# Row statistics of tiles 26 to 28 from accumulating ScalarE passes, and the last tile's maximum from its centred rows

## The chip, the core and the metric

The kernel runs on one core of a Trainium2 chip. The metric is the device time of one execution in microseconds, as the median of the runs.

## The reference

A transformer block on x of 8 batches x 512 rows x 512 columns, with a context of 77 rows a batch:

```
x = x + cross_attention(layernorm(x), ctx) @ Wo + bo        # 8 heads of 64
n = layernorm(x)                                            # over the 512 columns, eps 1e-5
s = sigmoid(clip_x) * max(abs(n)) / 127                     # one scale for the whole tensor
q = clip(round(n / s), -128, 127)
h = silu(s * q @ Wg') * (s * q @ Wu')                       # Wg', Wu', Wd' rounded to 8 bits by row
h is rounded in the same way, with one scale for the whole tensor
x = x + h' @ Wd'
```

What matters here is that the scale s needs the largest absolute value of n over all 4096 rows. No row can be rounded, and no product of the feed-forward part can start, before the last row of the attention part is normalised and its maximum is known.

## The kernel before, in words

The 4096 rows are 32 tiles of 128 rows. The attention part goes through the tiles in order, and tile n of the second normalisation takes these steps: `wo(n)` on TensorE gives the output projection; `residual(n)` (L607, VectorE) adds it to the row tile and writes `x1`; `second_stats` and `second_aggr` (L613, L617, VectorE) give mean and variance; `second_scale` (L621, L623, L625, GpSimd) gives the inverse deviation `r2` and the product `mr2` = -mean x `r2`; `normed(n)` (L631, ScalarE) writes `n2` = `x1` x `r2` + `mr2`, and a DMA of SyncE's queue stores it to DRAM (`n2_rows`); `largest(n)` (L637, VectorE) writes the tile's largest absolute value to a column of `amx`. The store of `x1` to the output tensor goes through the same SyncE queue. `x1` and `n2` have four buffers each (tile n uses buffer n mod 4), so `residual(n)` waits until the store of `x1` of tile n-4 has landed, and `normed(n)` until that of `n2` has.

The order of every engine's instructions is written out by hand: `add(engine, ...)` appends to the engine's list and gives a semaphore value, and an engine runs its list in order. `last_batch()` writes out tiles 22 to 27, and a loop behind it tiles 28 to 31. Between the two stand four small ScalarE operations (L1021, called dg here), which make diagonal matrices of weight scales. The last tile is normalised on VectorE in place of ScalarE (`last_normed`, L644). ScalarE meanwhile loads the activation table of Silu with a one-row activation (`warm`, L1036) and copies the spread weight scales out of PSUM (`sdb`, L219).

`PV(7, j)`, j = 0 to 3, are the last attention products. Each is taken out of PSUM in two parts, a high one by ScalarE (L565) and a low one by VectorE (L566), and part j of `wo(28)` waits for the low part j.

Then `whole_scale` makes the scale: VectorE reduces `amx` (L1061) and puts it on a diagonal (L1063), TensorE spreads it (L1065), VectorE makes the maximum, the scale and its inverse (L1068, L1070, L1073). `load_n2(b)` brings the four tiles of batch b back from DRAM into `n2b`, in four DMAs of 256 KB. `quant_y` (L1094 on ScalarE, for the very first tile L1091 on VectorE) scales and rounds, `quant_top` and `quant_low` (L1099, L1105) clip, `turn` (L1113) transposes on TensorE, and a copy to `nT` (L219 or L220) feeds the first products of the feed-forward part (`first_rows`, L1189). Their order on ScalarE: rounding of tiles 1 and 2 of batch 0, the copy of tile 0's transpose, rounding of tile 3. From there on `ffn` (L1137) keeps TensorE supplied with gate and up products of 88 chunks.

`P` is the buffer of the softmax rows with three slots. Slot 0 was last used by tile 30, slot 1 by tile 31. `mv1` holds the statistics of the first normalisation, `mv2` those of the second.

Of the kernel before, what the change touches and what calls it, by code (L numbers as in the profile page):

```python
# [5 lines left out]
class Chain:  # L6
# [8 lines left out]
    def add(self, engine, fn, waits=(), sig=None, by=1):  # L15
        need = []
        for tok in waits:
            if tok is None:
                continue
            name, value = tok  # L20
            if self.seen[engine].get(name, 0) < value:
                self.seen[engine][name] = value
                need.append((self.sems[name], value))
        sem = None
        if sig is not None:
            if sig not in self.sems:
                self.sems[sig] = self.ctx.enter_context(self.nc.semaphore(sig))
                self.count[sig] = 0
            sem = self.sems[sig]
            self.count[sig] += by  # L30
        self.queue[engine].append((need, fn, sem, by))
        return (sig, self.count[sig]) if sig is not None else None
# [30 lines left out]
def block_kernel(nc, x, xT, ctxT, Wq, Wk, Wv, Wo, bo, clip_x, clip_h, w_gate, w_up, w_down, out):  # L63
    f32, f32r, bf16 = mybir.dt.float32, mybir.dt.float32r, mybir.dt.bfloat16
    ALU, ACT, AX = mybir.AluOpType, mybir.ActivationFunctionType, mybir.AxisListType
    NB, L, H, D, I = 8, 77, 8, 512, 1408
# [7 lines left out]
    with ctx:  # L74
# [461 lines left out]
        def PV_rest(b):  # L536

            banks = []
            for j in range(2):
                at = state["use"] % 2  # L540
                state["use"] += 1
                banks.append((at, state["banks"][at], state["free"][at]))
            for k in range(2):
                banks.append((None, SP[:, 512 * k:512 * k + 512], (t_sub[min(4 * b + 4, NT - 1)],)))
            pv_at[b] = banks

            def fn(e):
                for i, (hv, hp) in enumerate(((0, 0), (0, 1), (1, 0))):
                    for j in range(4):
                        q = slice(32 * j, 32 * j + 32)  # L550
                        m = e.matmul(banks[j][1], vbd[q, hv, 4, :], pts[q, hp, 4, :], start=(i == 0), stop=False)
                return m
            add("pe", fn, [t_pl[4 * b + 3], t_vb[b], *(t for bank in banks for t in bank[2])], "qo_mm")
# [21 lines left out]
        def wo(n):  # L575
            b, t = n // 4, n % 4
            w = slice(t * 128, t * 128 + 128)
            free = {30: t_pl[31], 31: t_oss[7, 2]}[n] if n >= 30 else t_x1.get(n - 2)
            for j in range(4):
                def fn(e, j=j):  # L580
                    e.matmul(wo_bank(n), os_[:, 0, j, w], wos[:, 0, j, :], start=(j == 0), stop=False)  # L581
                    e.matmul(wo_bank(n), os_[:, 0, j, w], wos[:, 1, j, :], start=False, stop=False)  # L582
                    return e.matmul(wo_bank(n), os_[:, 1, j, w], wos[:, 0, j, :], start=False,  # L583
                                    stop=(j == 3))
                t_Wo[n] = add("pe", fn, [t_oss[b, j] if b == 7 else t_oss[b, 1], t_wol, free, t_c], "Wo_mm")
# [19 lines left out]
        def residual(n, engine="dve"):  # L605
            k = n % RR
            t_x1[n] = add(engine, lambda e: e.tensor_tensor(x1[:, k, :], wo_bank(n), xn[:, n % XR, :],  # L607
                                                           ALU.add),
                          [t_Wo[n], t_xb[n], t_x1s.get(n - RR), t_n2.get(n - RR)] + t_flat, "x1" if engine == "dve" else "x1_p")
            t_x1s[n] = dma("sp", out_v[n], x1[:, k, :], [t_x1[n]], f"st_x1_{k}")  # L610

        def second_stats(n):
            t_st2[n] = add("dve", lambda e: e.bn_stats(out=bn2[:, n % 2, :], in_=x1[:, n % RR, :]),  # L613
                           [t_x1[n]], "st2")

        def second_aggr(n):
            t_mv2[n] = add("dve", lambda e: e.bn_aggr(out=mv2[:, n, :], in_=bn2[:, n % 2, :]), [t_st2[n]],  # L617
                           "ag2")
# [10 lines left out]
        def normed(n):  # L629
            k = n % RR  # L630
            t_n2[n] = add("act", lambda e: e.activation(n2[:, k, :], x1[:, k, :], ACT.Identity,  # L631
                                                        bias=mr2[:, n:n + 1], scale=r2[:, n:n + 1]),
                          [t_r2[n], t_n2s.get(n - RR), t_am.get(n - RR)], "n2")
            t_n2s[n] = dma("sp", n2d[n], n2[:, k, :], [t_n2[n]], f"st_n2_{k}")

        def largest(n):
            t_am[n] = add("dve", lambda e: e.tensor_reduce(amx[:, n:n + 1], n2[:, n % RR, :], AX.X,  # L637
                                                           ALU.max, apply_absolute_value=True),
                          [t_n2[n]], "amx")

        def last_normed(n):

            k = n % RR
            t_n2[n] = add("dve", lambda e: e.tensor_scalar(n2[:, k, :], x1[:, k, :], mv2[:, n, 0:1], r2[:, n:n + 1],  # L644
                                                           ALU.subtract, ALU.mult),
                          [t_r2[n], t_n2s[n - RR], t_am[n - RR]], "n2_d")
            t_n2s[n] = dma("sp", n2d[n], n2[:, k, :], [t_n2[n]], f"st_n2_{k}")

        wg_v = w_gate.rearrange("(r p) n -> r p n", p=128)
# [276 lines left out]
        def last_batch():  # L926

            def second(n):
                second_stats(n)
                second_aggr(n)  # L930
                second_scale(n)

            normed(22)
            first_stats(31)
            first_aggr(31)
            first_scale(31)
            wo(23)
            residual(23)
            PV_rest(6)
            second(23)  # L940
            for j in (2, 3, 0, 1):
                PV(6, j)
            PT(28)
            S(29)
            S(30)
            PT_high(28)
            soft_max(29)
            soft_sub(29)
            load_vb(7)
            load_wgu(2)  # L950
            load_wgu(3)
            soft_exp(29)
            soft_max(30)
            soft_sub(30)
            PT_low(28)
            soft_exp(30)
            normed(23)
            soft_sum(29)
            soft_rec(29)
            soft_norm(29)  # L960
            wo(24)
            S(31)
            soft_sum(30)
            soft_rec(30)
            soft_norm(30)
            soft_max(31)
            soft_sub(31)
            soft_exp(31)
            wo(25)
            residual(24)  # L970
            PT(29)
            PT_high(29)
            soft_sum(31)
            soft_rec(31)
            soft_norm(31)
            PT_low(29)
            wo(26)
            residual(25)
            second(24)
            largest(21)  # L980
            first_bias(31)
            PT(30)
            PT_high(30)
            PT(31)
            PT_high(31)
            normed(24)
            PT_low(30)
            PT_low(31)
            state["free"][0] = state["free"][1] = (t_pl[30],)
            wo(27)  # L990
            residual(26)
            PV_rest(7)
            second(25)
            residual(27)
            largest(22)
            for j in range(4):
                PV(7, j)
                if j == 0:
                    normed(25)
            second(26)  # L1000
            second(27)
            largest(23)
            normed(26)

        for s in range(28):
            attend(s)
# [9 lines left out]
        gone = [t_S[31], t_q[7]]  # L1016


        for r in range(4):
            dgt = wraw[:, 0, r * 128:r * 128 + 128]  # L1020
            t_dg = add("act", lambda e, r=r, dgt=dgt: e.activation(dgt, identF[:, :], ACT.Identity,  # L1021
                                                                   scale=wsc[:, 22 + r:23 + r]),
                       [t_idF, t_wsc[25], t_wb[24], t_wb[25]], "dg")

        for n in range(28, NT):
            wo(n)
            normed(n - 1)
            residual(n)
            second_stats(n)
            second_aggr(n)  # L1030
            second_scale(n)
            for at in {28: (24, 25), 29: (26, 27), 30: (28,), 31: (29, 30)}[n]:
                largest(at)
            if n == 30:
                load_n2(0, gone + [t_n2s[tt] for tt in range(4)])
        add("act", lambda e: e.activation(warm[:, :], sge[0:1, :], ACT.Silu), [t_sge], "warm")  # L1036
        last_normed(31)
        largest(31)
        load_n2(1, gone + [t_n2s[4 + tt] for tt in range(4)])


        def spread_scale(e):
# [384 lines left out]
```

How the kernel before makes its waits and increments, by code:

```python
    def run(self, engine, e):  # L47
        for need, fn, sem, by in self.queue[engine]:
            for s, v in need:
                e.wait_ge(s, v)
            ins = fn(e)
            if sem is not None:
                ins.then_inc(sem, by)
```

## Time and profile before

| | us |
|---|---|
| median of 3 runs | 547.78 (546.44 to 548.42) |
| the profiled execution, its own time | 547.3 |
| its span | 545.5 |
| TensorE busy | 528.1 (97%) |
| VectorE busy | 475.3 (87%) |
| ScalarE busy | 294.2 (54%) |
| GpSimd busy | 231.8 (42%) |

The span runs from the first to the last instruction; the execution's own time has 1.8 us around it. Positions are in microseconds from the start of the span. An engine's share is an average over stages of different kinds: the attention part ends at about 298 us, the scale is made up to about 305 us, the feed-forward part follows. In square brackets behind a row stand the idle time of the engine in front of it and what ended that. A weight load of TensorE is listed apart from its product. One operation's duration can overlap the start of the next on the same engine, so the distance from start to start is often 0.1 us shorter than the duration.

### The profile page before, as it was taken

What the parts mean: (1) busy time and instruction counts of PE and PEld (TensorE: products, weight loads), DVE (VectorE), ACT (ScalarE), POOL (GpSimd) and SP (SyncE); (2) the same over time, 40 slices, a digit from 0 to 9 for tenths busy, and PEclk for the clock granted to TensorE, in tenths of its full rate; (3) what the DMA queues carried; (4) which work ended last, traced back from release to release, by engine and by line L of the source; (5) the groups of instructions that cost most, each with busy time, mean ns of one, the idle gap of its engine ahead of it and who ended that gap; (6) DMA issues with size and microseconds to landing.
All of it is one profiled execution on the core that took longest, in us unless ns stands there. A gap on an engine that the chain in (4) does not pass through costs nothing.

```text
span 545.5 us, 8102 instructions
## 1 busy us (share of the span) xinstructions
PE 528.1 (97%) x2740; PEld 355.9 (65%) x2740; DVE 475.3 (87%) x879; ACT 294.2 (54%) x414; POOL 231.8 (42%) x349
## 2 busy tenths in 40 slices
PE   8989889999999999999999899999999999999997
PEld 7868678787888878888788644444444445544444
DVE  4966988999989899898989799999999988899884
ACT  4834645556465654554534646555545533999500
POOL 4385858769596895856553000000000000055442
PEclk9999999999999999999999999999999999999999
DMA  8809375765668465545949955850442220399987
GB/s 315 275 41 301 92 210 171 226 215 160 214 212 272 143 216 178 178 129 165 203 88 313 282 122 242 283 141 22 116 117 44 72 38 5 123 328 234 159 106 127
DMA packets 82943, 93.83 MB, mean 172 GB/s; under 512 B 47085, under 2 KB 50157, under 8 KB 82645
## 3 DMA queue, kind: packets, MB, share of 16 engines
q1 hardware_dynamic: 77877, 84.13, 49.9%
q0 software_dynamic: 4320, 7.87, 9.6%
q10 hardware_dynamic: 704, 1.31, 0.7%
q8 instruction: 22, 0.36, 0.3%
q14 instruction: 20, 0.16, 0.1%
HBM read 47.51 MB, written 37.78 MB: 156 GB/s over the span
## 4 chain that ended last, share of the span: by engine, by line
PE 73%; DVE 12%; SPq 6%; DMA 3%; issue 2%; ACT 1%; POOL 1%; ACTq 0%; DVEq 0%; POOLq 0%
PE SP L1137 13%; PE QO L1137 13%; PE QO L192 5%; PE QO L194 4%; PE QO L193 4%; SPq L37 4%; PE SP L463 4%; PE QO L1294 4%; PE PTP L1294 3%; PE SP L1294 3%; SPq L41 2%; PE MI L583 2%; PE MI L582 2%; PE MI L581 2%; PE WOP L1294 2%
## 5 line engine op out<-in xcount | busy, mean ns | idle before, releaser
L45 POOL DMA_DIRECT2D out<-n2b x30 | 30.3, 1045 | 207.4 <-DVE n2b L1327 207.4
L1144 ACT ACTIVATE sil<-QO,fsc 128x512 f32<-128x512 f32 x87 | 59.8, 687 | 70.9 <-PE QO L1137 69.3
L1137 PE MATMUL SP<-nT,wgu 128*128 128x512 bf16 x340 | 87.3, 379 | 0.4
L1137 PE MATMUL QO<-nT,wgu 128*128 128x512 bf16 x340 | 87.3, 379 | 0.1
L1148 DVE SCALAR_TENSOR_TENSOR h<-SP,fsc,sil 128x512 f32<-128x512 f32 x87 | 65.1, 748 | 8.7 <-PE SP L1137 7.1
L504 POOL TENSOR_TENSOR PN<-P,rs 128x512 f32<-128x512 f32 x64 | 44.3, 714 | 50.2 <-DVE rs L496 50.2
L1151 DVE TENSOR_REDUCE hmx<-h 128x1 f32<-128x512 f32 x87 | 59.7, 686 | 3.0
L487 ACT ACTIVATE P<-P,r 128x616 f32<-128x616 f32 x32 | 26.0, 812 | 63.7 <-DVE P L483 63.7
L1137 PEld LDWEIGHTS SP<-nT,wgu 128*128 128x128 bf16 x340 | 32.9, 98 | 41.4 <-DVE h L1148 2.5
L1137 PEld LDWEIGHTS QO<-nT,wgu 128*128 128x128 bf16 x340 | 33.2, 98 | 40.2 <-ACT sil L1144 0.3
L192 PE MATMUL QO<-xTs,wqs 128*128 128x512 f32 x124 | 50.4, 407 | 2.3 <-DVE xTs L223 2.0
L1261 ACT ACTIVATE h<-h,magic,g 128x1536 f32<-128x1536 f32 (+2 forms) x38 | 47.8, 1350 | 3.3 <-DVE g L1073 3.3
L194 PE MATMUL QO<-xTs,wqs 128*128 128x512 f32 x124 | 48.5, 391 | 0.0
L193 PE MATMUL QO<-xTs,wqs 128*128 128x512 f32 x124 | 48.3, 390 | 0.0
L463 PE MATMUL SP<-kst,qs 128*128 128x154 f32 x248 | 38.1, 296 | 4.0 <-DVE P L483 1.8
L602 POOL TENSOR_TENSOR xn<-xn,bob 128x512 f32<-128x512 f32 x32 | 41.3, 1294 | 0.0
L686 ACT ACTIVATE wraw<-wraw,magic,wiv 128x512 f32<-128x512 f32 (+1 forms) x26 | 24.1, 928 | 31.2 <-DVE wiv L679 31.2
L463 PEld LDWEIGHTS SP<-kst,qs 128*128 128x128 f32 x248 | 34.5, 190 | 5.9 <-DVE P L483 2.2
L631 ACT ACTIVATE n<-x,mr,r 128x512 f32<-128x512 f32 x31 | 25.0, 808 | 15.5 <-POOL mr L625 15.5
L1264 DVE TENSOR_SCALAR wgu<-h 128x1536 bf16<-128x1536 f32 (+2 forms) x39 | 29.3, 757 | 1.2 <-ACT h L1261 0.7
L192 PEld LDWEIGHTS QO<-xTs,wqs 128*128 128x128 f32 x124 | 23.3, 188 | 7.8 <-issue 2.2
L493 DVE TENSOR_REDUCE sm<-P 128x8 f32<-128x616 f32 x32 | 25.1, 785 | 2.6 <-ACT P L487 1.7
(224 smaller groups left out, 1203.3 us busy)
## 6 DMA issues: line engine op xcount, KB each, us to landing
xTr<-in_xT SPq DMA_DIRECT2D x8, 1024.0 KB, 7.9
xn<-in_x SPq DMA_DIRECT2D x32, 256.0 KB, 3.8
out<-x SPq DMA_DIRECT2D x32, 256.0 KB, 2.9
n_rows<-n SPq DMA_DIRECT2D x32, 256.0 KB, 2.7
n2b<-n_rows SPq DMA_DIRECT2D x32, 256.0 KB, 3.8
out<-n2b POOLq DMA_DIRECT2D x30, 256.0 KB, 6.5
h_spill<-h SPq DMA_DIRECT2D x2, 2816.0 KB, 9.3
h<-h_spill SPq DMA_DIRECT2D x6, 768.0 KB, 7.2
```

Of the source, the lines that this page charges most:

```text
L192: e.matmul(ps, lh, rh, start=(i == 0), stop=False)
L193: e.matmul(ps, lh, rl, start=False, stop=False)
L194: m = e.matmul(ps, ll, rh, start=False, stop=(i == n - 1))
L463: m = e.matmul(o, qs[:, b % 2, j, w], kst[:, b, j, :], start=(j % 2 == 0), stop=True, skip_group_check=True)
L504: t_norm[n] = add("pool", lambda e, to=to, rb=rb, l0=l0, l1=l1: e.tensor_tensor(to, u[:, :, l0:l1], rb, ALU.mult), [t_rec[n], t_PT.get(n - ...
L602: t_xb[n] = add("pool", lambda e: e.tensor_tensor(xn[:, n % XR, :], xn[:, n % XR, :], bob[:, :], ALU.add), [t_bn1[n], t_bo], "xb")
L1137: m = e.matmul(ps, wv_[:, k, col:col + 128], nT[:, b % 2, :, k, :], start=(k == 0), stop=(k == 3))
L1144: t_sil[n] = add("act", lambda e: e.activation(sil[:, n % SR, :], gp, ACT.Silu, scale=fsc[:, ic:ic + 1]), [t_g[n], t_fs, t_h.get(n - SR)], ...
L1148: t_h[n] = add("dve", lambda e: e.scalar_tensor_tensor(out=hv, in0=up, scalar=fsc[:, 11 + ic:12 + ic], in1=sil[:, n % SR, :], op0=ALU.mult ...
L1151: t_hm[n] = add("dve", lambda e: e.tensor_reduce(hmx[:, n:n + 1], hv, AX.X, ALU.max, apply_absolute_value=True), [t_h[n]], "hmx")
L1261: a = add("act", lambda e: e.activation(hv, hv, ACT.Identity, bias=magic[:, :], scale=g2[:, 1, 1:2]), [t_g2] + ([t_back[b, p]] if b < 2 el ...
L1294: mm = e.matmul(ps, hq[:, i % 2, k, tt * 128:tt * 128 + 128], wd[:, k, :], start=(k == 0), stop=(k == NI - 1))
```

## The change

Three things are done. First, the statistics of tiles 26, 27 and 28 no longer come from `second_stats` and `second_aggr` on VectorE. `row_sum(n)` is a ScalarE pass over `x1` whose accumulator gives the row's sum; GpSimd makes the negative mean of it. `row_squares(n)` is a second ScalarE pass, Square with the negative mean as bias, whose accumulator gives the sum of squares; three GpSimd operations make `r2` and `mr2`. The full-size outputs of both passes go to slots 0 and 1 of `P` and are not read. Second, for tile 31 ScalarE writes centred rows (`last_centred`), VectorE takes their maximum and multiplies it by `r2` (`last_largest`), and ScalarE scales the rows behind the table load (`last_normed`). Third, orders move: `largest(24)` and `largest(25)` go to the end of `last_batch`, `load_n2(0)` goes behind `normed(30)`, `largest(29)` stays behind tile 31's statistics, and `load_n2(1)` goes ahead of the last tile's store.

```diff
--- before.py
+++ after.py
@@ -638,12 +638,56 @@
                                                            ALU.max, apply_absolute_value=True),
                           [t_n2[n]], "amx")
 
+        def row_sum(n):
+
+            t_st2[n] = add("act", lambda e: e.activation(P[:, 0, 0:512], x1[:, n % RR, :], ACT.Identity,
+                                                         accum_out=mv1[:, n, 0:1]),
+                           [t_x1[n], t_norm[30], t_r8[n]], "n2")
+            t_mv2[n] = add("pool", lambda e: e.tensor_scalar(mv2[:, n, 0:1], mv1[:, n, 0:1], -1.0 / D, 1.0,
+                                                             ALU.mult, ALU.mult), [t_st2[n]], "vb")
+
+        def row_squares(n):
+
+            t = add("act", lambda e: e.activation(P[:, 1, 0:512], x1[:, n % RR, :], ACT.Square,
+                                                  bias=mv2[:, n, 0:1], accum_out=mv1[:, n, 1:2]),
+                    [t_mv2[n], t_norm[31]], "n2")
+            t1 = add("pool", lambda e: e.tensor_scalar(vb[:, n:n + 1], mv1[:, n, 1:2], 1.0 / D, EPS,
+                                                       ALU.mult, ALU.add), [t], "vb")
+            t2 = add("pool", lambda e: e.tensor_tensor(r2[:, n:n + 1], vb[:, n:n + 1], mhalf[:, :],
+                                                       ALU.pow), [t1, t_mh], "r2")
+            t_r2[n] = add("pool", lambda e: e.tensor_scalar(mr2[:, n:n + 1], mv2[:, n, 0:1],
+                                                            r2[:, n:n + 1], 1.0, ALU.mult, ALU.mult),
+                          [t2], "mr2")
+
+        t_cen = {}
+
+        def last_centred(n):
+
+            k = n % RR
+            t = add("pool", lambda e: e.tensor_scalar(mr2[:, n:n + 1], mv2[:, n, 0:1], -1.0, 1.0,
+                                                      ALU.mult, ALU.mult), [t_mv2[n]], "mr2")
+            t_cen[n] = add("act", lambda e: e.activation(n2[:, k, :], x1[:, k, :], ACT.Identity,
+                                                         bias=mr2[:, n:n + 1]),
+                           [t, t_x1[n], t_n2s[n - RR], t_am[n - RR]], "n2")
+            t1 = add("pool", lambda e: e.tensor_scalar(vb[:, n:n + 1], mv2[:, n, 1:2], EPS, 1.0,
+                                                       ALU.add, ALU.mult), [t_mv2[n]], "vb")
+            t_r2[n] = add("pool", lambda e: e.tensor_tensor(r2[:, n:n + 1], vb[:, n:n + 1], mhalf[:, :],
+                                                            ALU.pow), [t1, t_mh], "r2")
+
+        def last_largest(n):
+
+            t = add("dve", lambda e: e.tensor_reduce(amx[:, n:n + 1], n2[:, n % RR, :], AX.X,
+                                                     ALU.max, apply_absolute_value=True), [t_cen[n]], "amx")
+            t_cen["max"] = t
+            t_am[n] = add("dve", lambda e: e.tensor_tensor(amx[:, n:n + 1], amx[:, n:n + 1], r2[:, n:n + 1],
+                                                           ALU.mult), [t, t_r2[n]], "amx")
+
         def last_normed(n):
 
             k = n % RR
-            t_n2[n] = add("dve", lambda e: e.tensor_scalar(n2[:, k, :], x1[:, k, :], mv2[:, n, 0:1], r2[:, n:n + 1],
-                                                           ALU.subtract, ALU.mult),
-                          [t_r2[n], t_n2s[n - RR], t_am[n - RR]], "n2_d")
+            t_n2[n] = add("act", lambda e: e.activation(n2[:, k, :], n2[:, k, :], ACT.Identity,
+                                                        scale=r2[:, n:n + 1]),
+                          [t_r2[n], t_cen[n], t_cen["max"]], "n2")
             t_n2s[n] = dma("sp", n2d[n], n2[:, k, :], [t_n2[n]], f"st_n2_{k}")
 
         wg_v = w_gate.rearrange("(r p) n -> r p n", p=128)
@@ -989,18 +1033,22 @@
             state["free"][0] = state["free"][1] = (t_pl[30],)
             wo(27)
             residual(26)
+            row_sum(26)
             PV_rest(7)
             second(25)
             residual(27)
             largest(22)
+            row_squares(26)
             for j in range(4):
                 PV(7, j)
                 if j == 0:
                     normed(25)
-            second(26)
-            second(27)
+            row_sum(27)
             largest(23)
             normed(26)
+            row_squares(27)
+            largest(24)
+            largest(25)
 
         for s in range(28):
             attend(s)
@@ -1016,27 +1064,46 @@
         gone = [t_S[31], t_q[7]]
 
 
+        def second(n):
+            second_stats(n)
+            second_aggr(n)
+
+        wo(28)
+        residual(28)
+        normed(27)
+        row_sum(28)
         for r in range(4):
             dgt = wraw[:, 0, r * 128:r * 128 + 128]
             t_dg = add("act", lambda e, r=r, dgt=dgt: e.activation(dgt, identF[:, :], ACT.Identity,
                                                                    scale=wsc[:, 22 + r:23 + r]),
                        [t_idF, t_wsc[25], t_wb[24], t_wb[25]], "dg")
-
-        for n in range(28, NT):
-            wo(n)
-            normed(n - 1)
-            residual(n)
-            second_stats(n)
-            second_aggr(n)
-            second_scale(n)
-            for at in {28: (24, 25), 29: (26, 27), 30: (28,), 31: (29, 30)}[n]:
-                largest(at)
-            if n == 30:
-                load_n2(0, gone + [t_n2s[tt] for tt in range(4)])
+            if r == 1:
+                row_squares(28)
+        largest(26)
+        largest(27)
+        wo(29)
+        normed(28)
+        residual(29)
+        second(29)
+        second_scale(29)
+        largest(28)
+        wo(30)
+        normed(29)
+        residual(30)
+        second(30)
+        second_scale(30)
+        wo(31)
+        normed(30)
+        load_n2(0, gone + [t_n2s[tt] for tt in range(4)])
+        residual(31)
+        second(31)
+        last_centred(31)
+        largest(29)
+        largest(30)
+        last_largest(31)
         add("act", lambda e: e.activation(warm[:, :], sge[0:1, :], ACT.Silu), [t_sge], "warm")
+        load_n2(1, gone + [t_n2s[4 + tt] for tt in range(4)])
         last_normed(31)
-        largest(31)
-        load_n2(1, gone + [t_n2s[4 + tt] for tt in range(4)])
 
 
         def spread_scale(e):
```

## Rows read from the trace of the kernel before

**Rows 1.** Busy time of each engine in one stretch; PE, PEld, DVE, ACT, POOL, clock, DMA.
```profile
311.00:460.00 149.00, 148.49 (x697) 67.12 (x695) 137.12 (x229) 79.14 (x115) 0.00 (x0) 1.00 0.39 115
```
**Rows 2.** VectorE in order of time: start, duration, line, operation, [idle before].
```profile
291.25 0.69 DVE L607 TENSOR_TENSOR x<-WOP,xn 128x512 f32<-128x512 f32 x1 [0.29 <-DMA out<-x]
...
298.12 0.18 DVE L617 BATCH_NORM_AGGREGATE mv<-bn 128x2 f32<-128x6 f32 x1
298.22 0.65 DVE L637 TENSOR_REDUCE amx<-n 128x1 f32<-128x512 f32 x1
298.79 0.68 DVE L607 TENSOR_TENSOR x<-SP,xn 128x512 f32<-128x512 f32 x1
...
300.23 0.18 DVE L617 BATCH_NORM_AGGREGATE mv<-bn 128x2 f32<-128x6 f32 x1
...
301.73 0.55 DVE L644 TENSOR_SCALAR n<-x,mv,r 128x512 f32<-128x512 f32 x1
...
303.03 0.19 DVE L1061 TENSOR_REDUCE gcol<-amx 128x1 f32<-128x32 f32 x1
...
304.96 0.49 DVE L1091 TENSOR_SCALAR n2b<-n2b,g 128x512 f32<-128x512 f32 x1
```
**Rows 3.** GpSimd in order of time, the three operations of tile 30's scale.
```profile
298.38 0.19 POOL L621 TENSOR_SCALAR vb<-mv 128x1 f32<-128x1 f32 x1 [1.51 <-DVE mv L617]
298.66 0.55 POOL L623 TENSOR_TENSOR r<-vb,mhalf 128x1 f32<-128x1 f32 x1
299.31 0.27 POOL L625 TENSOR_SCALAR mr<-mv,r 128x1 f32<-128x1 f32 x1
```
**Rows 4.** ScalarE in order of time, around the change.
```profile
285.08 0.60 ACT L565 ACTIVATE os<-QO 128x512 fp32r<-128x512 f32 x1 [3.10 <-PE QO L561]
285.58 0.81 ACT L631 ACTIVATE n<-x,mr,r 128x512 f32<-128x512 f32 x1
286.28 0.58 ACT L565 ACTIVATE os<-QO 128x512 fp32r<-128x512 f32 x1
286.76 1.08 ACT L565 ACTIVATE os<-SP 128x512 fp32r<-128x512 f32 x2
...
291.64 1.26 ACT L1021 ACTIVATE wraw<-identF,wsc 128x128 f32<-128x128 f32 x4
...
299.62 0.81 ACT L631 ACTIVATE n<-x,mr,r 128x512 f32<-128x512 f32 x1 [1.89 <-POOL mr L625]
300.45 1.28 ACT L1036 ACT_TABLE_LOAD   x1
301.74 0.20 ACT L1036 ACTIVATE warm<-sge 1x2 f32<-1x2 f32 x1
...
304.95 1.52 ACT L1094 ACTIVATE n2b<-n2b,magic,g 128x512 f32<-128x512 f32 x2 [2.53 <-DVE g L1073]
```
**Rows 5.** TensorE in order of time: last product of tile 31, first feed-forward products.
```profile
297.79 0.40 PE L583 MATMUL SP<-wos,os 128*128 128x512 f32 x1
...
307.38 0.40 PE L1189 MATMUL QO<-nT,wgu 128*128 128x128 bf16 x4
```
**Rows 6.** SyncE's queue in order of time: batch 0's loads, tile 30's store.
```profile
298.79 1.80 SPq L37 DMA_DIRECT2D n2b<-n_rows  x4
300.64 0.43 SPq L37 DMA_DIRECT2D n_rows<-n  x1
```
**Rows 7.** DMA issues, median us to landing: first, second, third load of batch 0.
```profile
n2b<-n_rows SPq DMA_DIRECT2D x1, 256.0 KB, 2.7
n2b<-n_rows SPq DMA_DIRECT2D x1, 256.0 KB, 4.9
n2b<-n_rows SPq DMA_DIRECT2D x1, 256.0 KB, 5.2
```
**Rows 8.** The same view, loads of batch 2 at 323.4 and 325.7 us.
```profile
n2b<-n_rows SPq DMA_DIRECT2D x1, 256.0 KB, 3.4
n2b<-n_rows SPq DMA_DIRECT2D x1, 256.0 KB, 4.3
```

## The prediction

> **What bounds the kernel now.** I read the busy shares first, then the chain of waits, then each engine in order of time from 284 to 312 us. From 311 to 460 us TensorE is busy for 148.5 of 149.0 us [rows 1], so whatever moves the start of the feed-forward part should move the end by as much. The start hangs on the scale. VectorE is what makes the scale late: from `residual(28)` at 291.25, which a landing DMA releases [rows 2], it runs on without a gap to `last_normed`, while TensorE has its last projection product at 297.79 [rows 5] and `residual(31)` starts at 298.79, straight behind `largest(28)` [rows 2]. ScalarE and GpSimd are idle between their steps (1.89 and 1.51 us in front of tile 30's) [rows 3, 4]. Behind `residual(31)` come 1.44 us of statistics, 1.50 us of aggregate, three GpSimd operations and the step to the next engine, 1.30 us of `last_normed` and `largest(31)` to the reduction at 303.03, and 1.93 us to the first rounding at 304.96 [rows 2].
>
> **Prices.** From start to start: statistics and aggregate 0.83 us a tile on VectorE (1.44 less 0.61 of the residual); `largest` 0.57; a two-pointer normalisation 0.81, its follower on ScalarE 0.70 later (285.58 to 286.28); a pass without pointer 0.60; one dg 0.3 (1.26 for four); aggregate to `normed` 1.50, of which 1.24 from the first GpSimd operation [rows 2 to 4]. `row_sum` has no pointer operand, so 0.6; `row_squares`, `last_centred` and the new `last_normed` have one, so 0.7, between 0.60 and 0.81.
>
> No row shows an accumulator written out by ScalarE. Call its price a, added to the pass and to the engine's next start. It can be nothing (0), and I bound it above by 0.6, another pass over the row. The nearest row is the smallest ScalarE operation, 0.20 us for `warm` [rows 4], since what is written is one number a row. I take a = 0.2.
>
> **Part 1, tiles 26 to 28.** VectorE is rid of 3 x 0.83 = 2.5 us, but the work comes back as latency on another path, which I follow for a = 0.2. A tile's new path is `row_sum`, mean on GpSimd, `row_squares`, three GpSimd operations, `normed`.
>
> Tile 26 costs nothing: its two passes and the mean between take about 1.5 + 2a = 1.9 us, and ScalarE is idle for 3.10 us in front of the copy at 285.08 [rows 4]. If they ran over, each 0.1 would delay the copies, `wo(28)` and so TensorE by 0.1.
>
> Tile 27: `row_sum(27)` follows the last copy at 287.75 (two from 286.76 take 1.08, 0.1 of it overlapped). `normed(26)` starts 0.5 + a later, `row_squares(27)` 0.71 behind that, at 289.17. Its sum is seen after 0.75 + a, then 1.24 to `normed(27)`: 291.36. ScalarE is free at 292.07. `residual(28)` stays at 291.25, since a DMA releases it, and ends at 291.96. So both are ready together.
>
> Tile 28: `row_sum(28)` 292.07; plus 0.5 + a and two dg (0.6): `row_squares(28)` 293.37; plus 0.75 + a + 1.24: `normed(28)` 295.56; plus 0.85: `largest(28)` 296.41; plus 0.57: `residual(30)` 296.98. Here is the new wait. VectorE, behind `residual(28)` at 291.96, has two `largest` (1.14), `residual(29)` with its statistics (1.44 + 0.10) and reaches `largest(28)` at 294.6; there it stands for 1.8 us, with `residual(30)`, `residual(31)` and all behind queued. Before, `normed(28)` had long been done. Then 1.44 + 0.10 give `residual(31)` at 298.52, 0.27 us earlier than before. TensorE's product would allow about 298.2.
>
> **Part 2, the last tile.** The aggregate of tile 30 is at 298.42, `normed(30)` 1.50 later at 299.92, `last_centred` behind it on ScalarE at 300.63 (its bias is ready by 300.5). Its reduction can start 0.75 later, 301.38; `largest(29)` and `largest(30)` end just before. The reduction takes 0.72, the multiplication by `r2` 0.2 (as the scale's small operations), and the reduction over `amx` starts at 302.3, against 303.03. The first rounding could start at 304.2, against 304.96. So VectorE's side gains 0.7 us.
>
> ScalarE's tail is just inside the cover: table load at 301.2 (1.28, then the next operation at once), `warm` 0.2, `last_normed` 0.7, `sdb` 0.5 (a pass as at 285.08) give 303.9, before the scale at 304.1. The wait of `last_normed` on the maximum (302.1) is over by then. Behind it only `sdb` and the roundings queue.
>
> **Part 3, the loads of batch 0.** They are what is late next. Before, the four were issued from 298.79, ahead of tile 30's store [rows 6]. Now they stand behind this store, which needs `normed(30)`: store at 300.75, loads at 301.2, 301.65, 302.1 and 302.55, 2.4 us later than before. The first load landed 2.7 us after its issue, the second 4.9, the third 5.2 [rows 7]. ScalarE must round tiles 1 and 2 before it copies tile 0's transpose, and the first product at 307.38 [rows 5] waits for that copy, 1.36 us behind the start of tile 2's rounding (0.71 to the copy, 0.60 for it, 0.05 to TensorE). Before, this start was set by the engine and the transpose; now it is the landing of tile 2. Two ends: with the lags of the same loads before, tile 2 lands at 307.3, and the first product starts at about 308.7, 1.3 us late. With 2.7 us for each (302.1 + 2.7 = 304.8), nothing waits and the whole 0.7 is kept. Loads of later batches, with nothing in front of them but a transpose, took 3.4 and 4.3 [rows 8]: tile 2 at 305.5 to 306.4, the first product at 306.9 to 307.8, so 0.5 earlier to 0.4 later. Now too less traffic is ahead of the loads (one store instead of two within a microsecond), which is why I take this middle: a change of 0.
>
> SyncE's queue is passed as well by `load_n2(1)`, now ahead of tile 31's store. Issued from 303.5 to 305.3 and 5.3 us under way at most, they land by 310.6, and batch 1 is first rounded behind the first Silu, which needs all of the first products (about 4 us of them from 307.4); tile 31's rows are wanted only in batch 7. The transposing load of `wd` waits for that store, and is needed only after 460 us. I count both at nothing; if that cover were gone, the 2.3 us of four issues would show.
>
> **The sum.** Maximum path -0.7, loads +0.7 (0 to +2.0): 0.0. The profiled execution took 547.3 with a span of 545.5, and the median is 547.78; I give the shift to the median: 547.7.
>
> **Rivals.** *Late loads make it slower.* One mechanism: tile 2 of batch 0 lands at 307.3, ScalarE's queue holds tile 0's copy behind it, +1.3 us: 549.1. It decides from a lag of about 3.8 us, where landing plus 1.36 passes 307.38. For it: the lags of these very loads. Against it: the lighter traffic.
>
> *The full gain.* Loads land in time, a = 0.2: 547.1. With a = 0 the path is shortened by another 0.5 (two of the four accumulator writes are covered by `residual(28)`): 546.5. For it is the 2.7 of the first load.
>
> *Accumulation is dear.* Four accumulator writes in a row lie on the path to `largest(28)`, so each 0.1 of a costs 0.4. At a = 0.37 the gain on the scale is gone; at 0.6 the reduction is at 304.4, and the loads go with it: +1.4 to +3.4, 549.1 to 551.2. Nothing in the trace speaks for it.
>
> *Square costs a table load.* The trace has a load where Silu is first used, 1.28 us with the next operation straight behind it [rows 4]. If Square were not in the set of Exp, one such load would come in front of `row_squares(26)`, over its cover by about 1.0: the copies and TensorE are 1.0 later, and the reduction over `amx` at 303.3, +0.3 by itself, with loads +1 to +2: 549.2. The Trainium skill (ScalarE: Activation LUTs, Table sets: the hidden batching unit) says that cheap functions, of which it lists relu, copy, identity and abs, are in every set. Square isn't in that list. The same page (What ACT_TABLE_LOAD costs) adds 1.38 us of drain to a load; the trace does not show it here, and with it the case would come out 1.4 higher.
>
> **How the numbers follow.** No shift within 0.5 us: 0.45. Late loads: 0.25. Full gain: 0.18. Dear accumulation: 0.05. Table load: 0.04. Something else, such as a lowered clock in a longer gap of TensorE: 0.03. The runs of before spread over 2 us, so the median itself is good to about 0.7: the range is 546.5 less 0.4 to 549.1 plus 0.4, so 546.1 to 549.5. What can be told from no change is about 0.5%, 2.7 us; only the worst ends of the last three cases reach it upward. Faster 0.04, within 0.5% 0.90, slower 0.06.
>
> **What would show it.** Right: a wait of VectorE in front of `largest(28)` of 1.5 to 2.3 us; `residual(31)` near 298.5; the reduction over `amx` near 302.3; accumulator writes of about 0.2; loads of batch 0 from about 301.2 and ScalarE's second and third rounding waiting for them; one table load. Wrong: the wait missing (a near 0), a table load ahead of Square, or the first product before 306.7 or after 308.5.

## The result, and the profile after

The changed kernel takes 551.03 us (550.7 to 551.64, 4 runs), the kernel before 547.5 (546.44 to 548.42, 4 runs). The ratio is 1.0065, with a 95% interval of 1.0049 to 1.008. It is 3.5 us slower, outside the range of 546.1 to 549.5. The ratios, here and below, leave out three single executions that ran far longer (773.41 us in the third experiment, 1099.17 us in the seventh, 556.33 us of the kernel before in the last two), while the medians include them. The profiled execution took 551.64 with a span of 549.8; that of before had 545.5.

Executions differ by up to a microsecond in what comes ahead of the change. So I count from the start of the low part of PV(7, 0), L566 on VectorE: 285.71 us before, 285.98 after. The span then falls into five pieces, each counted from the end of the one above.

| us | before | after | difference |
|---|---|---|---|
| to the first low part | 285.71 | 285.98 | +0.27 |
| from there to the reduction over `amx` | 17.32 | 16.81 | -0.51 |
| to the first feed-forward product | 4.35 | 6.22 | +1.87 |
| to the first product of 512 columns | 4.31 | 5.67 | +1.36 |
| to the end of the span (the tail) | 233.81 | 235.12 | +1.31 |

**The path to the scale** went nearly as forecast: it gained 0.51 us, against 0.7. ScalarE in order of time, kernel after:

```profile
292.70 0.63 ACT L643 ACTIVATE P<-x 128x512 f32<-128x512 f32 x1 [0.45 <-DVE x L607]
293.23 0.19 ACT L643 ACTIVATION_READ_ACCUMULATOR P<-x 128x1 f32 x1
293.33 0.68 ACT L1077 ACTIVATE wraw<-identF,wsc 128x128 f32<-128x128 f32 x2
293.91 0.71 ACT L651 ACTIVATE P<-x,mv 128x512 f32<-128x512 f32 x1
294.53 0.19 ACT L651 ACTIVATION_READ_ACCUMULATOR P<-x,mv 128x1 f32 x1
294.62 0.68 ACT L1077 ACTIVATE wraw<-identF,wsc 128x128 f32<-128x128 f32 x2
296.03 0.81 ACT L631 ACTIVATE n<-x,mr,r 128x512 f32<-128x512 f32 x1 [0.73 <-POOL mr L658]
```

The accumulator is written out by an instruction of its own of 0.19 us, and the next operation starts 0.10 behind it. No table load stands ahead of Square. VectorE has the new wait:

```profile
291.97 0.69 DVE L607 TENSOR_TENSOR x<-WOP,xn 128x512 f32<-128x512 f32 x1 [1.14 <-DMA out<-x]
...
296.87 0.69 DVE L637 TENSOR_REDUCE amx<-n 128x1 f32<-128x512 f32 x1 [1.48 <-ACT n L631]
...
299.03 0.69 DVE L607 TENSOR_TENSOR x<-SP,xn 128x512 f32<-128x512 f32 x1
...
302.79 0.19 DVE L1128 TENSOR_REDUCE gcol<-amx 128x1 f32<-128x32 f32 x1
```

These answer to [rows 2]: the wait in front of `largest(28)` is 1.48 us, and the reduction over `amx` comes at 302.79 against 303.03.

The size of this gain differs from one execution to the next. The kernels below that keep the accumulating passes have the same order of work up to `residual(28)`, apart from spare operations that fit into idle time. Where the store of tile 24 landed early (first, fifth and seventh experiment), `residual(28)` started 4.95 or 4.96 us behind the first low part and the reduction over `amx` came at 16.23 to 16.26. Where it landed late (the changed kernel, sixth and tenth experiment), the two stood at 5.83 to 5.99 and 16.66 to 16.81. The two profiles of the path as it was before give 17.32 and 17.46 (second experiment). So the gain is 0.5 to 1.2 us, and differences of less than about 0.5 us between two single profiles say nothing on this path unless `residual(28)` starts equally early in both.

**The loads of batch 0** are next. SyncE's queue, ScalarE and TensorE in order of time, against [rows 4 to 6]:

```profile
301.26 0.32 SPq L37 DMA_DIRECT2D n_rows<-n  x1
301.83 1.77 SPq L37 DMA_DIRECT2D n2b<-n_rows  x4
```
```profile
305.39 0.81 ACT L1161 ACTIVATE n2b<-n2b,magic,g 128x512 f32<-128x512 f32 x1 [0.94 <-DMA n2b<-n_rows]
307.66 0.81 ACT L1161 ACTIVATE n2b<-n2b,magic,g 128x512 f32<-128x512 f32 x1 [1.46 <-DMA n2b<-n_rows]
308.38 0.58 ACT L219 ACTIVATE nT<-PTP 128x512 bf16<-128x512 bf16 x1
```
```profile
307.05 0.40 PE L1180 MATMUL PTP<-identB,qb 128*128 128x128 bf16 x4 [0.60 <-DVE qb L1172]
309.01 0.61 PE L1256 MATMUL QO<-nT,wgu 128*128 128x128 bf16 x4 [1.56 <-ACT nT L219]
```

The rounding of tile 2 waits for its load, tile 0's copy is queued behind it, and TensorE waits for the copy. Landings of the second and third load (issues at about 302.3 and 302.7), to be read against [rows 7]:

```profile
n2b<-n_rows SPq DMA_DIRECT2D x1, 256.0 KB, 3.2
n2b<-n_rows SPq DMA_DIRECT2D x1, 256.0 KB, 4.9
```

**The clock.** Busy time of each engine by stretch; the third number from the end is TensorE's granted clock:

```profile
308.00:310.00 2.00, 0.99 (x10) 0.99 (x11) 1.36 (x4) 1.66 (x3) 0.00 (x0) 0.62 0.98 370
310.00:312.00 2.00, 2.00 (x22) 2.00 (x20) 0.56 (x3) 0.60 (x1) 0.00 (x0) 0.52 0.46 174
312.00:314.00 2.00, 2.00 (x39) 2.00 (x37) 0.42 (x1) 0.06 (x1) 0.00 (x0) 1.00 0.04 9
```

The granted clock is given as a share of 2.4 GHz. Around the 1.56 us in which TensorE stood, it fell to half, 1.2 GHz, and stayed there until 312: 22 products in 2 us, then 39. Before, the clock was 1.00 in all these stretches.

**The tail.** Waits of TensorE from 311 to 460 us; before there were none.

```profile
PE QO L1204 <- DMA nT<-qb: 1.0, 2, 0.6
```

They belong to the transposing loads of batches 2 and 5, issued at 345.59 and 403.30. A transposing load brings the four rounded tiles of a batch, transposed, into `nT`. These two took 5.2 us to landing, the other five 4.2 or 4.3 (before, all seven 4.3):

```profile
nT<-qb SPq DMA_TRANSPOSE x1, 5.2
```

From the issue of such a load to the issue of the next it took 19.73 and 19.66 us behind these two, against 18.99 before, which is the whole 1.31 us of the tail within 0.1. In the stretches 349.4 to 349.6 and 407.0 to 407.2, that is 3.7 to 4.0 us behind their issue, the DMA view has one packet of an instruction queue, that is, of code:

```profile
q14 instruction: 1, 0.01, 9.7%
```

Before, the corresponding packets came in the stretches from 341.4 and from 398.4, 1.0 to 1.2 us ahead of the issues at 342.61 and 399.59:

```profile
q14 instruction: 1, 0.01, 10.7%
```

### The profile page after: what moved, and what is told of

Read it like the earlier page. It is cut to its first block, busy times and chain, and to the rows that moved or that the text cites. A ratio compares the mean times of both kernels' runs of the same rounds, so it can differ in the third digit from the quotient of the medians.

```text
span 549.8 us, 8110 instructions
## 1 busy us (share of the span) xinstructions
PE 529.0 (96%) x2733; PEld 356.9 (65%) x2740; DVE 472.8 (86%) x873; ACT 299.7 (55%) x428; POOL 232.2 (42%) x352
## 3 DMA queue, kind: packets, MB, share of 16 engines
q10 hardware_dynamic: 704, 1.31, 0.7%
## 4 chain that ended last, share of the span: by engine, by line
PE 76%; DVE 10%; DMA 6%; SPq 3%; issue 2%; ACT 2%; POOL 1%; ACTq 0%; DVEq 0%
PE SP L1204 12%; PE QO L1204 11%; PE QO L192 5%; PE SP L463 5%; PE QO L194 4%; PE QO L193 4%; PE PTP L1361 3%; PE QO L1361 3%; PE SP L1361 3%; SPq L37 3%; PE MI L583 2%; PE MI L581 2%; PE MI L582 2%; DMA nT<-qb 2%; PE PTP L516 2%
```

## The experiments

Each is given with its own runs of the kernel before, taken on the same chip.

**1. Loads back in their place**, the rest of the change kept:

```diff
         second_scale(30)
+        load_n2(0, gone + [t_n2s[tt] for tt in range(4)])
         wo(31)
         normed(30)
-        load_n2(0, gone + [t_n2s[tt] for tt in range(4)])
```

> The changed kernel with one line moved: the four loads of batch 0 stand ahead of tile 30's normalised rows in SyncE's queue again, as before. Theory 1 (late loads, then TensorE at half clock): the loads land before the scale is there, the second rounding of ScalarE waits for none, the first feed-forward product comes at about 306.7 to 307.3, no stretch has a granted clock under 0.9, and the time is 0.3 to 1.0 us BELOW the kernel before (546.5 to 547.2). Theory 2 (the accumulating passes or the new last tile cost the 3.5 us in a way that I have not seen): the time stays at 550 to 551. Between the two, 548 to 549.5: the loads are one cause of two.

547.92 against 547.32, ratio 1.0019 (1.0001 to 1.0037): most of the 3.5 us is gone, yet there is no gain over the kernel before, and the forecast time of 546.5 to 547.2 is missed. The profile tells why: from the first low part, the reduction over `amx` comes at 16.23, the first product at 20.59, the first 512-column product at 24.89 (before 25.98), with the clock at 1.00, but the tail is 235.15. Theory 1 held up to the first products and missed the tail. This is where I first saw that the tail has a cause of its own, with the same two loads at 5.2 us.

**2. Loads late in the kernel before**, nothing else changed:

```diff
-            if n == 30:
-                load_n2(0, gone + [t_n2s[tt] for tt in range(4)])
...
             normed(n - 1)
+            if n == 31:
+                load_n2(0, gone + [t_n2s[tt] for tt in range(4)])
             residual(n)
```

> The kernel before with only the loads of batch 0 moved behind tile 30's store; statistics and last tile as before. Theory 1: store of tile 30 at about 300.5, loads from 300.9, third load lands near 307.0, first product at 308.3 instead of 307.4, and if TensorE's clock falls to half there, another 1 to 1.5 us: 548.5 to 550.5, slower than before by 1 to 3. The price of the loads alone is smaller than in the changed kernel, since the store comes 0.8 us earlier. Theory 2: 547.5, no difference.

548.55 against 547.32, 1.0020 (1.0008 to 1.0032). The first 512-column product comes at 27.01, 1.03 later than before, 0.89 of it between the reduction over `amx` and the first product; the tail is 233.80.

```profile
308.59 0.40 PE L1189 MATMUL QO<-nT,wgu 128*128 128x128 bf16 x4 [0.91 <-ACT nT L219]
```

TensorE stood for 0.91 us in front of its first product, and here the clock stayed at 1.00. So late loads alone cost about 1 us, and the lowered clock is not tied to every such gap.

**3. A filled gap**: the changed kernel with products that nobody reads.

```diff
         turn(0, 1, "dve")
+        keep_clock(8)
         first_rows(0)
```

> The changed kernel with 8 small products more on TensorE, behind the transposes of tiles 0 and 1, where it stood for 1.56 us (307.45 to 309.01); their output is not read. The late loads stay. Theory 1 in two parts: if the half clock from 309.0 to 311.9 comes from that idle stretch, it goes, the clock stays at 1.00, and 1.2 to 1.5 us of the 3.5 go with it: 549.5 to 549.8. If the lowered clock has another cause, or if only the wait counts: 551, as the changed kernel. The fillers themselves take 1.9 us and could run past 309.0 by at most 0.3.

550.34 against 547.32, 1.0052 (1.0035 to 1.0069), which overlaps the changed kernel's 1.0065. The forecast was 549.5 to 549.8. Its profile is of the execution of 773.41 us, so no stretch can be read beside the others. It settles nothing by itself; the seventh experiment asks again.

**4. The last tile's part alone**, with statistics of tiles 26 to 28 on VectorE and loads as before:

```diff
-            row_sum(26)
-            row_squares(26)
-            row_sum(27)
-            row_squares(27)
+            second(26)
+            second(27)
...
-        row_sum(28)
-                row_squares(28)
+        second(28)
+        second_scale(28)
...
         second_scale(30)
+        load_n2(0, gone + [t_n2s[tt] for tt in range(4)])
         wo(31)
         normed(30)
-        load_n2(0, gone + [t_n2s[tt] for tt in range(4)])
```

> Tiles 26 to 28 with statistics on VectorE as before, loads as before; of the change the last tile's centred rows, its maximum and the new order of the maxima stay. By the prices read before: aggregate of tile 31 at 300.2, centred rows at 300.5 behind normed(30), their maximum at 301.5, reduction over amx at 302.4 against 303.03: 0.6 us less than before, 546.9. If the accumulating passes of tiles 26 to 28 are worth something, the first kernel of this call is below this one by up to 0.3; if they cost, above. Theory 2 in the form that the last tile's part is what costs: 549 or more.

546.82, 0.9984 (0.9966 to 1.0003). The reduction over `amx` is at 16.49, 0.83 earlier than before. With the accumulating passes it comes at 16.23 to 16.81, on both sides of this. So the last tile's part alone brings most of what is gained on this path, and what the passes of tiles 26 to 28 add is not shown. The first 512-column product gains only 0.40: the second rounding waits 0.69 us for its load, which is now late for the earlier scale. The tail is 233.78, so the last tile's part does not lengthen it.

**5. Seven spare VectorE operations**, loads back. Counted in the traces with semaphore instructions, VectorE has 1116 instructions before and 1109 after; this brings it to 1116 again.

```diff
+        def spare(k0, k1):
+            for k in range(k0, k1):
+                add("dve", lambda e, k=k: e.tensor_scalar_mul(mx8[:, k // 8, k % 8:k % 8 + 1],
+                                                              mx8[:, k // 8, k % 8:k % 8 + 1], 1.0))
         wo(28)
+        spare(0, 3)
         residual(28)
...
+        spare(3, 7)
         largest(28)
```

> The first experiment (loads of batch 0 back in their place) with 7 tiny VectorE operations more (one column of a dead softmax buffer times 1.0), three in VectorE's idle time ahead of residual(28), four in that ahead of largest(28). The changed kernel has 7 instructions fewer on VectorE than the kernel before, and in it and in the first experiment two of the transposing loads of nT (batches 2 and 5) take 5.2 us instead of 4.3, with an 8 KB packet of the instruction queue 0.6 us ahead of their landing; TensorE waits 0.5 us each time. Theory A (the VectorE count sets when its code is fetched, and the fetch delays a load that TensorE is about to need): with 7 back, all seven transposing loads take 4.3 us, no wait of TensorE in 311 to 460 us, from the first 512-wide product to the end of the span 233.8 us instead of 235.1, and the time is 546.2 to 546.8, below the kernel before by 0.5 to 1.1. Theory B (something else in the accumulating kernels lengthens the tail, such as chance or placement): tail 235.1, 547.9, as the first experiment.

546.65 against 547.68, 0.9989 (0.9974 to 1.0005). The seven transposing loads take 4.2 to 4.3 us, TensorE has no wait from 311 to 460, and the tail is 233.74. The first 512-column product is at 24.91, as without the spare operations. Theory A holds. The code packet comes in the stretch from 340.8 to 341.0, about 1.1 us ahead of the issue at 341.99.

**6. The changed kernel with the same seven**:

> The changed kernel, loads late as it has them, with the same 7 tiny VectorE operations more. Theory A: tail 233.8 instead of 235.1, time 549.4 to 549.9, that is 1.2 to 1.6 below the changed kernel's 551.0; the half clock between 309 and 312 us stays. Theory B: 551.0.

549.31 against 547.68, 1.0035 (1.0017 to 1.0053). Tail 233.78, all seven loads 4.3 us. The loads of batch 0 and the half clock stay (0.86, 0.50 and 0.79 from 308 to 314 us), with the first 512-column product at 28.79.

```profile
308.69 0.40 PE L1264 MATMUL QO<-nT,wgu 128*128 128x128 bf16 x4 [1.65 <-ACT nT L219]
```

Here the clock is 1.00 through the gap of 1.65 us and falls only behind the first products: it is 0.72 from 309 to 310 us.

**7. The same, and the gap filled**:

```diff
         turn(0, 1, "dve")
+        keep_clock(8)
         first_rows(0)
```

> The same, and 8 small TensorE products more behind the transposes of tiles 0 and 1, in the stretch in which TensorE waits for the late load; their output is not read. If the half clock comes from that idle stretch, the granted clock is 1.00 throughout, the first 32 small feed-forward products take 4.1 us instead of 5.6, and the time is 1.2 to 1.5 below the kernel without these fillers: 548.1 to 548.6, which is the price of the late loads alone, 0.8 to 1.3 over the kernel before. If not: as that kernel.

548.81 against 547.68, 1.0017 (0.9998 to 1.0036). TensorE around the gap, and the stretch behind it:

```profile
306.46 2.00 PE L1129 MATMUL WOP<-ones 128*128 128x128 f32 x16
308.30 0.39 PE L1264 MATMUL QO<-nT,wgu 128*128 128x128 bf16 x4
```
```profile
308.00:310.00 2.00, 2.00 (x36) 1.99 (x35) 0.99 (x4) 0.57 (x2) 0.00 (x0) 1.00 0.92 350
310.00:312.00 2.00, 2.00 (x40) 2.00 (x38) 0.42 (x1) 0.36 (x2) 0.00 (x0) 1.00 0.04 12
```

The clock stays at 1.00, the first products take 4.30 us instead of 5.93 in the sixth experiment, and the first 512-column product is at 26.90: 1.89 earlier than there, 0.92 later than before. But this does not show that the filling kept the clock up, because ScalarE was earlier too:

```profile
306.19 0.81 ACT L1169 ACTIVATE n2b<-n2b,magic,g 128x512 f32<-128x512 f32 x1 [0.81 <-DMA n2b<-n_rows]
306.91 0.58 ACT L219 ACTIVATE nT<-PTP 128x512 bf16<-128x512 bf16 x1
```

The third load took 4.3 us in this execution, against 4.9 in the sixth experiment, and tile 0's copy ended at 307.49. The first product followed such a copy by 0.05 elsewhere, so I estimate that without fillers it would have started at 307.54, behind a gap of 0.91 us, the length at which the clock stayed up in the second experiment. The fillers held it until 308.30, 0.76 later. So 1.89 is 1.63 of clock, 0.40 of an earlier scale and a loss of 0.14 in between, and of the 0.92 left over the kernel before 0.76 is the price of the fillers. The times, 1.0017 and 1.0035, overlap.

**8. Seven fewer VectorE instructions in the kernel before**:

```diff
-            t_wsc[i] = add("dve", lambda e: e.tensor_scalar_mul(wsc[:, at:at + 1], wmx[:, i:i + 1],
-                                                                1.0 / 127.0), [t_wmx[i]], "w_sc")
+            own = 3 <= i < 10
+            t_wsc[i] = add("pool" if own else "dve", lambda e: e.tensor_scalar_mul(wsc[:, at:at + 1], wmx[:, i:i + 1],
+                                                                1.0 / 127.0), [t_wmx[i]], "w_sc_p" if own else "w_sc")
```

> The kernel before with 7 tiny VectorE operations (the weight scales of tiles 3 to 9) given to GpSimd; nothing else. Theory A: VectorE has 7 instructions fewer, so the transposing loads of batches 2 and 5 take 5.2 us, TensorE waits about 0.5 us for each, and the tail from the first 512-wide product is 235.1 instead of 233.8; the time goes to about 548.7, and any stall of VectorE for GpSimd's scale in the attention part adds up to 1 us more, which the tail does not hold. Theory B: tail 233.8.

555.08, 1.0138 (1.0117 to 1.0159). The forecast of the time is a miss: the attention part grew far more than by 1 us. In the profile the first low part is at 292.73, 7 us later than before. This profiled execution took 557.92, 2.8 over the median, and its granted clock was 0.97 over the first 100 us, so the edit itself costs less than these 7. In the tail theory A holds: the transposing loads of batches 2 and 5 take 5.2 and 5.1 us, the others 4.3 or 4.4, and the tail is 235.61; of the 1.8 over the kernel before, 0.5 falls behind the last of these loads and has no explanation here. The waits of TensorE (the second number is how many; none such before):

```profile
PE QO L1138 <- DMA nT<-qb: 1.0, 2, 0.5
```

The code packet is at 355.0, 3.8 us behind the issue at 351.20.

**9. `largest(28)` later**, in the fifth experiment, and the loads one tile earlier:

```diff
         second_scale(29)
+        load_n2(0, gone + [t_n2s[tt] for tt in range(4)])
         spare(3, 7)
-        largest(28)
         wo(30)
...
         second_scale(30)
-        load_n2(0, gone + [t_n2s[tt] for tt in range(4)])
+        largest(28)
```

> The fifth experiment (loads back, 7 spare VectorE operations) with largest(28) behind the statistics of tile 30 instead of ahead of residual(30), and the loads of batch 0 one tile earlier still. If VectorE's wait of 1.4 us in front of largest(28) held up the end, residual(31) comes earlier; I expect that TensorE's last projection product holds it already (it ends within 0.1 us of residual(31) in the fifth experiment), so residual(31) stays, normed(30) comes 0.8 us earlier and stops being in front of last_centred, and the reduction over amx comes 0.1 to 0.2 earlier, 16.1 us after the first low part instead of 16.26. Time 546.3 to 546.7, not to be told from the fifth experiment. If the wait was on the path: 0.5 us or more less.

546.5 against 547.2, 0.9988 (0.9977 to 0.9999).

```profile
297.93 0.69 DVE L607 TENSOR_TENSOR x<-SP,xn 128x512 f32<-128x512 f32 x1 [0.52 <-PE SP L583]
```

Tile 31's residual now waits for TensorE and starts at 12.51 from the first low part, as in the fifth experiment. So VectorE's 1.4 us wait had not held it up there, where `residual(28)` was early as well. The reduction over `amx` is at 16.13 against 16.26, as `normed(30)` no longer stands right in front of `last_centred` on ScalarE. Where `residual(28)` is late, as in the changed kernel, this experiment says nothing.

**10. The fifth experiment again**:

> The fifth experiment again, word for word, on the chip of this call: its first measurement gave 0.9989 of the kernel before, with an interval that still holds 1. Theory A says 0.9980 (1.1 us earlier first 512-wide product, same tail). An interval wholly under 1 would show the gain; one around 1 leaves it open.

546.0 against 547.2, 0.9982 (0.9969 to 0.9995). This interval lies under 1; the tail is 233.75. The first 512-column product is at 25.35 in this profile, 0.63 earlier than before and not 1.1: `residual(28)` waited 0.86 us for tile 24's store. The version with loads back and seven spare operations is about 1 us faster than the kernel before, and 4 to 5 us faster than the change as made.

## Why the prediction was wrong

**Right: the path to the scale.** The passes of tile 26 fitted into ScalarE's gap: the first copy started 0.27 us later, as everything in front of it did. The wait in front of `largest(28)` was forecast at 1.8 and measured at 1.48 us. `residual(31)` came at 299.03, 298.76 on the clock of before, against a forecast of 298.52. The reduction over `amx` gained 0.51 instead of 0.7. The missing 0.2 is there: `residual(28)` waited for the landing of tile 24's store until 291.97, by the first low part 0.45 later than before, and a part of this was hidden. The prediction had it stay where it was. With this store early, the same path gained 1.06 to 1.09 (first, fifth and seventh experiment). The accumulator's price a = 0.2 was a little high: 0.10 on the engine's next start, about 0.15 on what waits for the sum.

**Failed: "loads +0.7".** From the reduction over `amx` to the first product it was +1.87, near the upper end of the 0 to +2.0 given. The first product came at 309.01, past the 308.5 named as a sign of being wrong. The step chose the middle between two ends, tile 2 landing at 305.5 to 306.4. It landed at 307.6. The reason given, that less traffic was ahead of the loads, did not hold: the third load took 4.9 us with one store in front, 5.2 before with two. The end that I had worked out from these very rows, first product 1.3 late, is what came: 1.36 by the first low part. The nearest row was at hand, and I went by transfers of a quieter stretch. The scatter is wide: the third load took 4.9 to 5.0 us in three of the profiles with late loads and 4.3 in the seventh experiment. The second experiment gives the price in the kernel before: 0.89 us on the same piece.

**Failed: a gap without a price.** A lowered clock stood under "something else" with a chance of 0.03 and no figure. The rows had the clock at 1.00 through gaps of 1.4 us of TensorE, but these lay between fillers. With a gap of 1.56 us in front of them and little done by TensorE since 305.4, the first products ran at half clock, 1.36 us lost; the same came with the gap of 1.65 us (sixth experiment). Where there is no such gap the clock is 1.00 (first, fifth, ninth, tenth), and behind gaps of 0.45 to 0.91 us it is 0.99 or 1.00 (fourth, eighth, second). So the half clock went with the loads put back, and it comes with the two longest of these gaps only. That filling the gap would save it is not shown: the one profile with fillers had an early load.

**Failed: "should move the end by as much".** TensorE was busy to 99.7% from 311 to 460 us [rows 1], so I took the rest of the span as rigid. It was rigid to shifts in time: the tail is 233.74 to 233.81 in eight profiled executions whose first 512-column products lie up to 4.4 us apart. But it was not rigid to the number of VectorE's instructions. With 7 fewer, two transposing loads land 0.9 us later, just past the moment when TensorE needs them. Removing 7 (eighth) brings the delay, adding 7 (fifth, sixth) takes it away. That the delay comes from the code packet that falls into their flight is what the timing fits in all eleven profiles that can be read. They have 77 transposing loads of `nT`. A code packet began behind the issue of seven of these and ahead of their landing, and these seven took 5.1 to 5.4 us; the other 70 took 4.2 to 4.4. Whose code the packet carries, and why one packet costs 0.9 us, is not shown.

The rivals: "late loads make it slower" (0.25) was the right mechanism, at +1.36 against my +1.3. Half clock and tail together added 2.7, for which I had no rival. Late loads alone, at +1.36, would have kept the time inside the range. "Accumulation is dear" and "Square costs a table load" did not occur: the trace has two table loads in all, before and after, and none between them. The sentence of the Trainium skill (ScalarE: Activation LUTs, Table sets: the hidden batching unit) that cheap functions are in every set does not name Square; that Square needs no load behind Exp is what this trace shows.

Two sums in the prediction are off without bearing on the forecast. By its own 0.4 us for each 0.1 of a, a = 0.6 gives the reduction at 303.9 and not 304.4, +0.9 and not +1.4 without the loads. And the lag from which late loads decide is 3.9 us (307.38 less 1.36 less 302.1), not 3.8.

## What to carry to other kernels

When a step is moved behind a store in a DMA queue, count the transfers behind it at the lags that these same transfers show in the profile, not at those of a quieter place, and ask what waits behind the operation that waits for them. A gap on TensorE is priced twice, once as the wait and once as what the clock gives behind it, until a run shows otherwise. A profile with the fix in it must also be asked what the gap would have been without the fix, since a DMA's landing can differ by half a microsecond between executions. A change that removes instructions can also move where the later code is fetched: compare the landings of repeated transfers one by one between two profiles before calling a long steady stage unchanged.

## What I had not expected

Seven operations of 0.1 us, placed in idle time of VectorE and without effect on any value, took 1.3 to 1.4 us off the tail (235.15 to 233.74). The transposing load takes 4.3 us in nearly all its instances in all kernels, and 5.1 or 5.2 where a code packet comes 3.7 to 4.0 us behind its issue. In one more kernel (the seventh experiment) the load of batch 1, issued at 322.32, took 5.4 us, with no harm, as TensorE needed it later. A larger packet, of another instruction queue, falls into it as well, between 324.7 and 324.8:

```profile
nT<-qb SPq DMA_TRANSPOSE x1, 5.4
```
```profile
q8 instruction: 1, 0.02, 58.0%
```
